# Perceiver layer kernel: attention energies and self scores in tensor tiles of 32 rows by 64 columns, self outputs made transposed, a new bank layout and new step orders

## The reference

```python
x = x + xattn(layernorm(x), ctx, ctx, mask, Wq, bq, Wk, bk, Wv, bv, Wo, bo)
#   energy = einsum('bhqd,bhkd->bhqk', Q, K) / sqrt(16); masked to -1e20
#   softmax(energy) @ V, heads side by side, @ Wo.T + bo
x = x + attn(layernorm(x), W_Q, W_K, W_V, W_O)
#   rope(q), rope(k); scores = einsum('bhqd,bhkd->bhqk', q, k) / sqrt(16), causal
#   softmax(scores) @ v, heads side by side, @ W_O.T
x = x + ffn(layernorm(x), router_w, w0_kernel, w1_kernel, wo_kernel)
#   top-2 gates, dispatch to 8 experts, gelu(x w0) * (x w1), @ wo, combine
```

## Time and profile before

| | |
|---|---|
| time, three runs | 659.47 us median (658.26 to 662.77) |
| span of the profiled execution | 666.9 us (its own device time is not listed apart) |
| mean granted TensorE clock | 0.928 of full speed |
| busy share of PE, DVE, ACT, POOL | 92%, 69%, 49%, 31% |
| one full step of four batches | 43.8 us |
| tail | 82 us |

### The profile page before, as it was taken

The page is one execution under the profiler, slowest core; times in us unless marked ns, Lnnn a source line. Parts: engine busy times, 40 slices in busy tenths (PEclk is TensorE's granted clock), DMA queues, the critical chain, the costliest instruction groups (busy, mean ns, idle before and its releaser), DMA issues.

```text
span 666.9 us, 14695 instructions
## 1 busy us (share of the span) xinstructions
PE 614.8 (92%) x4639; PEld 571.1 (86%) x4639; DVE 457.8 (69%) x1190; ACT 329.8 (49%) x836; POOL 208.0 (31%) x327
## 2 busy tenths in 40 slices
PE   2889999999999999999999889758999996999996
PEld 2868889899898898998988778748999996999995
DVE  3415667567776685677666755555999975999984
ACT  3336665545544545455444220335566655666662
POOL 0410221103113021021130210224666654666760
PEclk9989999989999999899998965656999998999998
DMA  8011111100001011010000070002555563645501
GB/s 266 24 47 34 32 33 33 32 18 30 21 17 31 16 31 31 16 31 0 0 1 1 8 247 0 0 1 95 161 189 159 161 212 106 191 158 191 160 1 63
DMA packets 38408, 47.51 MB, mean 71 GB/s; under 512 B 2414, under 2 KB 30036, under 8 KB 38356
## 3 DMA queue, kind: packets, MB, share of 16 engines
q1 hardware_dynamic: 38356, 46.82, 22.5%
HBM read 45.77 MB, written 1.05 MB: 70 GB/s over the span
## 4 chain that ended last, share of the span: by engine, by line
PE 82%; DVE 8%; ACT 4%; issue 4%; DMA 1%; SPq 0%; POOL 0%; DVEq 0%; ACTq 0%
PE bank L208 17%; PE bank L209 16%; PE bank L210 16%; PE bank L503 7%; PE bank L585 5%; PE bank L471 5%; PE bank L489 4%; PE bank L608 4%; PE bank L429 2%; PE bank L840 1%; ACT Pr L908 1%; PE bank L724 1%; PE bank L644 1%; DVE PT L1218 1%; DVE sc L1313 1%
## 5 line engine op out<-in xcount | busy, mean ns | idle before, releaser
L908 ACT ACTIVATE Pr<-Sc,nmax 128x257 f32<-128x257 f32 x128 | 64.2, 503 | 102.5 <-DVE nmax L1183 102.5
L208 PE MATMUL bank<-XT_lo,W_hi 128*128 (+1 forms) x352 | 101.5, 288 | 5.8 <-DVE W_lo L1523 4.4
L209 PE MATMUL bank<-XT_hi,W_lo 128*128 (+1 forms) x352 | 100.8, 286 | 0.0
L210 PE MATMUL bank<-XT_hi,W_hi 128*128 (+1 forms) x352 | 100.5, 286 | 0.0
L1697 POOL TENSOR_TENSOR W_lo<-raw,W_hi 128x256 fp32r<-128x256 f32 (+1 forms) x88 | 86.2, 979 | 7.0
L1523 DVE TENSOR_TENSOR W_lo<-raw,W_hi 128x512 fp32r<-128x512 f32 (+1 forms) x91 | 72.6, 802 | 5.0 <-ACT W_hi L1023 1.3
L1183 DVE CUSTOM_DVE_ANT_0 Sc<-bank,mask_add 128x257 f32<-128x257 f32 x128 | 49.2, 422 | 38.6 <-PE bank L471 37.4
L208 PEld LDWEIGHTS bank<-XT_lo,W_hi 128*128 128x128 f32 (+1 forms) x352 | 67.4, 191 | 6.4 <-issue 6.4
L1553 DVE TENSOR_TENSOR hid_lo<-hid,hid_hi 128x256 fp32r<-128x256 f32 (+1 forms) x88 | 69.3, 787 | 3.0 <-ACT hid_hi L1105 2.9
L209 PEld LDWEIGHTS bank<-XT_hi,W_lo 128*128 128x128 f32 (+1 forms) x352 | 67.3, 191 | 0.0
L210 PEld LDWEIGHTS bank<-XT_hi,W_hi 128*128 128x128 f32 (+1 forms) x352 | 67.1, 191 | 0.0
(11 more groups left out here) (210 smaller groups left out, 1572.1 us busy)
## 6 DMA issues: line engine op xcount, KB each, us to landing
raw<-in_L_ffn_w_kernel SPq DMA_DIRECT2D x32, 512.0 KB, 4.6
ctx_raw<-in_ctx SPq DMA_DIRECT2D x32, 256.0 KB, 2.7
raw<-in_L_ffn_wo_kernel SPq DMA_DIRECT2D x16, 512.0 KB, 5.7
raw<-in_L_ffn_w_kernel SPq DMA_DIRECT2D x16, 344.0 KB
raw<-in_L_ffn_wo_kernel SPq DMA_DIRECT2D x8, 256.0 KB
x_sb<-in_x SPq DMA_DIRECT2D x1, 1024.0 KB, 5.8
out<-fin SPq DMA_DIRECT2D x8, 128.0 KB, 1.8
raw<-in_L_ffn_wo_kernel SPq DMA_DIRECT2D x8, 88.0 KB
```

Source lines behind the costliest of these rows:

```text
L208: pe.matmul(dst, a_hi, b_lo, start=first, stop=False)
L209: pe.matmul(dst, a_lo, b_hi, start=False, stop=False)
L210: return pe.matmul(dst, a_hi, b_hi, start=False, stop=last)
L908: ac.activation(Pr[:, r % 2, g, 0:SC], Sc[:, r % 2, g, 0:SC], ACT.Exp, bias=nmax[:, r % 2, g:g + 1], scale=-1.0, accum_out=Pr[:, r % 2, g, ...
```

## The change

Five things change together.

1. **Energies.** HP = 2 heads per block of 32 rows. `energies(b, r)` issues all of a batch at once: 8 matmuls of 32 rows by 64 columns, into banks 0 to 3, two halves of the output partitions each. `Qb` is half as large.
2. **Scores.** The same tiles: 32 matmuls in one call, into columns 258 and up of banks 0 to 3 (`spare`). Half 0 of the probabilities and the turned self probabilities use the same columns, so PE waits before each of them until the last reader is done.
3. **Self outputs.** The values are padded with zeros to 32 columns (`Vm`) and used as weights, so the product comes out transposed; `turn_self` and `normalise` go. The probabilities are divided before they are turned: `add_probs` on VectorE (128x512 reduction and a reciprocal), `scale_probs` on GpSimd (128x512).
4. **Banks.** 0 to 3 energies and `spare`; 4 turned context and half 1; 5 keys and values both; 6 front; 7 back, and in its upper half the outputs.
5. **Orders.** Self probabilities are turned and spread at u = 3 instead of u = 2, self outputs are one call at u = 3; the tail has a new order. In the head, four weights are loaded in two transfers each.

```diff
         def values(b, r):
...
-            if beyond(b, 3):
-                pe.wait_ge(sm["o_read"], b - 2)
-            elif b > 0:
-                pe.wait_ge(sm["v_ready"], b)
+            pe.wait_ge(sm["k_ready"], b + 1)
...
-        def energies(b, r, pair):
+        def energies(b, r):
...
-            if beyond(b, 1) or pair:
-                pe.wait_ge(sm["s_read"], 4 * b + 2 * pair)
-            for g in range(2):
-                last = pe.matmul(bk[3 + g][:, 0:SC], Qb[64 * g:64 * g + 64, r % 2, pair, :, :],
-                                 KT[64 * g:64 * g + 64, r % 2, pair, 0:SC], start=True, stop=True)
...
+            if beyond(b, 1):
+                pe.wait_ge(sm["s_read"], 4 * b)
+            if beyond(b, 2):
+                pe.wait_ge(sm["pt0_ready"], b - 1)
+            for c in range(KH):
+                for g in range(G):
+                    rows = slice(S * g, S * g + S)
+                    last = pe.matmul(bk[g][64 * c:64 * c + 64, 0:SC], Qb[rows, r % 2, c, :, :], KT[rows, r % 2, c, 0:SC],
+                                     start=True, stop=True)
             last.then_inc(sm["s_made"], 1)
...
         def turn_probs(b, r, t):
...
                 pe.wait_ge(sm["p_ready"], 4 * b + 4)
+                pe.wait_ge(sm["s_read"], 4 * min(b + 2, B) if isinstance(b, int) else 4 * b + 8)
...
+        def outputs(b, r, t):
...
+            if exists(t, TT):
+                pe.wait_ge(sm[("b_x2", "c_yT", "c_lg", "b_x2")[(r + 2) % 4]], t + 1)
...
+            for b in range(BT):
+                for c in range(KH):
+                    for g in range(G):
+                        rows = slice(S * g, S * g + S)
+                        last = pe.matmul(spare(t)[64 * c:64 * c + 64, g, b * S:(b + 1) * S], qTb[rows, c, b, :, :],
+                                         kT[rows, c, b * S:(b + 1) * S], start=True, stop=True)
+            last.then_inc(sm["b_s_made"], 1)
...
+        def after_self(t, scored):
...
+            if scored:
+                pe.wait_ge(sm["b_scaled"], t + 1)
+            else:
                 pe.wait_ge(sm["b_pT_act"], t + 1)
                 pe.wait_ge(sm["b_pT_dve"], t + 1)
...
+            for k in range(KH):
+                for a in range(HP):
+                    for q in range(BT):
+                        h = NH // KH * k + HP * q + a
+                        last = pe.matmul(back(t)[S * q:S * q + S, k * P:(k + 1) * P],
+                                         values_of(t)[:, h // HP, 3 * DH * a:3 * DH * a + S], PTd[:, h // HG, h % HG, :, :],
+                                         start=a == 0, stop=a == HP - 1)
...
+                if u == 1:
+                    scores(j - 2)
...
+                if u == 3:
+                    self_outputs(j - 2)
                 values(b + 1, (u + 1) % 4)
...
-        def maxima(b, r, pair):
+        def maxima(b, r, pair, t):
...
+            if pair == 0 and r % 2 and exists(t, TT):
+                ve.wait_ge(sm["b_s_made" if r == 1 else "b_pT_made"], t + 1)
...
+        def add_probs(t):
...
+            ve.tensor_reduce(sum2[:, :], flat(pr2), X, ALU.add).then_inc(sm["b_sum"], 1)
+            ve.wait_ge(sm["b_sum"], t + 1)
+            ve.reciprocal(inv2[:, :], sum2[:, :]).then_inc(sm["b_inv"], 1)
...
+        def scale_probs(t):
...
+            po.tensor_tensor(probs, probs, inv2[:, :].unsqueeze(2).broadcast_to([P, NH, S]), ALU.mult).then_inc(sm["b_pn"], 1)
```

More of the change, by code:

```diff
@@ L51, in constants @@
     slot = np.broadcast_to(np.arange(E * CAP), (P, E * CAP))
-    parts = [ident, before, np.repeat(cos, 2, 1), sin, -sin, causal, block, expert, first_slot, slot]
+    parts = [ident, before, np.repeat(cos, 2, 1), sin, -sin, np.tile(causal, (1, BT)), block, expert, first_slot, slot]
     table = np.concatenate([np.asarray(t, np.float32) for t in parts], 1)
@@ L251, in halves, with weight_in, positions_at, spare @@
         return ap.rearrange("p (k n) -> p k n", k=KH)
+    def weight_in(i):
+        return 16 * KH if i in BY_HEAD else 16
     def front(t):
-        return bk[1] if isinstance(t, int) and t == TT - 1 else bk[2]
+        return bk[4] if isinstance(t, int) and t == TT - 1 else bk[6]
     def back(t):
-        return bk[5] if isinstance(t, int) and t == TT - 1 else bk[6]
+        return front(t) if isinstance(t, int) and t >= TT - 2 else bk[7]
+    def positions_at(k):
+        return bk[(7, 4)[k]]
+    def spare(t):
+        at_ = SC + 1 if not isinstance(t, int) or t < TT - 2 else 2 * P if t == TT - 2 else 3 * P
+        return bank[:, 0:G, at_:at_ + P]
     def values_of(t):
-        return Vs[:, int(isinstance(t, int) and t == TT - 1)]
+        return Vm[:, int(isinstance(t, int) and t == TT - 1)]
+    BY_HEAD = (0, 1, 4, 5)
     BATCHES = [(0, TT - 2), (TT - 2, TT)]
@@ L634, in turn_router @@
             pe.wait_ge(sm["c_y"], t + 1)
+            if back(t) is bk[7]:
+                pe.wait_ge(sm["o_read"], B if isinstance(t, int) and t == TT - 3 else BT * t + 3 * BT - 1)
             for k in range(KH):
@@ L711, in positions @@
             pe.wait_ge(sm["r_chosen"], k + 1)
-            pe.matmul(bk[0][:, 0:2 * n], before, chosen[:, :, t0:t1, :], start=True, stop=True)
-            pe.matmul(bk[0][:, 2 * n:3 * n], ones[:, :], chosen[:, 0, t0:t1, :], start=True, stop=True)\
+            if k == 0:
+                pe.wait_ge(sm["o_read"], B)
+            at_ = positions_at(k)
+            pe.matmul(at_[:, 0:2 * n], before, chosen[:, :, t0:t1, :], start=True, stop=True)
+            pe.matmul(at_[:, 2 * n:3 * n], ones[:, :], chosen[:, 0, t0:t1, :], start=True, stop=True)\
               .then_inc(sm["r_pos_made"], 1)
@@ L1655, in step @@
                 elif u == 2:
+                    scale_probs(j - 2)
                     power(j - 1, "b")
```

328 lines of the change are left out of this document (157 added, 171 removed).

## The result

| | before | changed |
|---|---|---|
| time, four runs each | 661.12 us (658.26 to 667.95) | 679.38 us (674.4 to 684.25) |
| the changed kernel again, second series | 662.44 us | 672.43 us |
| profiled span | 666.9 us | 672.6 us |
| mean granted clock in it | 0.928 | 0.933 |
| full step | 43.83 us | 44.48 us |

The change makes the kernel slower: the ratio is 1.025 (95% interval 1.0185 to 1.0308) in the first series and 1.016 (1.0106 to 1.0221) in the second. The forecast was 668 us with a range of 648 to 692. The eight runs of the changed kernel fall into two groups, five of 670.7 to 675.2 us at a granted clock of 0.933 to 0.946 and three of 683.1 to 684.3 us at 0.920 to 0.922, so that the median of 679.38 us is the middle between two and two; the profiled execution (674.4 us) is of the first group.

A forecast was written before the change was run, and what follows sets the result against it. PE was taken to bound the loop, as long as VectorE's and ScalarE's answers stay hidden. First batches +8, steps +3.6, tail -3 and head +0.5 gave +9 us, 668 us on the median; range 648 to 692.

The forecast's parts named there:

- The plain batch: Loop: stalls of 1.1 us before the transposes and 0.6 before the values make a batch 8.5 us, against 7.52.
- The full step: Four batches of the loop: 35.4 us of PE work plus 9.1 of stalls, 44.5 against 43.8; six steps +3.6.
- the 0.10 us that I charged for leaving the row tiles: Energies on PE: each pair of calls was taken to cost about 0.10 us extra for leaving the row tiles twice.
- Energies: PE, each batch: the new call takes 0.6 us, 0.75 with entering and leaving; 0.75 less per batch, 3.0 per step.
- Scores: PE, each step: 64 records in 1.6 us, bounds 0.9 and 6.8; 2.9 us less per step.
- self outputs: PE, each step: 32 records in 1.1 us with entering and leaving, instead of 3.5; 2.2 us less per step.
- Rival (b): PE tiles: column halves run one after the other, much slower, 690 to 704 us; chance 0.15.
- The first eight batches: Start of the loop: waits for maxima and key copy add 1.0 us to each batch, +8 us.
- The head: Before the loop: two more transfers ahead of biases and x delay the first matmul, +0.5 us, 0 to +1.5.
- The tail: After the loop: shorter scores and self outputs of z against new waits, about -3 us, from -8 to +1.
- Rival (a): Loop: VectorE's and ScalarE's answers stay hidden under PE work (covers hold), so faster, 645 us; chance 0.25.
- Rival (c): PE's clock: stalls drop it to 1.2 GHz in part of the loop, about 680 us; chance 0.10.

The follow-up runs named there:

- the context turned twice: Kernel before the change with each batch's four transposes of the context issued twice: 670.35 us, ratio 1.0097.
- the maxima together: Changed kernel with a batch's last two maxima on VectorE right behind its first two, ahead of split context and output copies: 630.29 us, ratio 0.9525.

## Why the prediction was right, point by point

**The direction and the mechanism were right.** The plain batch was forecast at 8.5 us with stalls of 1.1 and 0.6 us; it takes 8.70 with 1.14 and 0.4 (the transposes' own stretch is a little longer than I had it). The chain behind it is shown by four runs: cut it at the maxima and 42 us go, cut it at the key copy and 10 us go, lengthen PE's work off the chain and the step stays, lengthen it at the chain's head and the batch grows by as much.

**The full step** was forecast at 44.5 and is 44.48, which is luck in part, for two errors cancel: I had 35.4 us of work and 9.1 of stalls, and it is 36.76 and 7.7. The waits I listed are there but for the output projection's (0.3), most of them smaller: x of tile j-3 0.3 for 0.6, the transposes at u = 0 and u = 2 2.4 for 2.9, the cross projection's 0.5 for 0.7, the transposes at u = 1 1.1 for 1.4, keys' copies 0.6 for 1.0, the spread self probabilities 1.1 for 1.2; the q and k projection's is larger, 1.2 for 1.0. One I had not is the logits' (0.5 us for the output copies). Some of the surplus of work is a matter of counting: the last matmul ahead of a wait counts as 0.28 us of PE, one that is followed at once as 0.12. And the 0.10 us that I charged for leaving the row tiles isn't there: behind the transposes of the kernel before, which use the whole array, the first matmul of the values is as long (0.36 us, 89.34) as the first of the keys is behind the energies (0.38).

**Tiles.** Energies 0.62 us for a forecast of 0.6. Scores 0.84 for 1.6, a little under the lower bound of 0.9, and self outputs 1.08 for 1.1. Rival (b), column halves one after the other, did not happen. The rule in the Trainium skill ("TensorE: Matmul & The Clock Gate", Part 3, The mechanism) that a weight load overlaps matmuls only of another row group would have given 1.0 us or more for the energies and about 3.4 for the self outputs, whose four column tiles all use the same rows; the runs disagree with it as far as time goes: 0.62 us and 1.08. So they do with the estimate by the overhead per matmul that the Trainium skill gives ("TensorEngine Tiling (Array Packing)", Instruction Overhead; 1.6 us for 64 records): 64 records start within 0.84 us, so that overhead is not paid one after another across tiles.

**The first eight batches** were forecast at +8 and cost +10.6. Batch 0 alone costs 3.5 of it: it has no transposes ahead of its values, so its wait for the key copy is 2.7 us instead of 0.4, and behind that wait PE ran 3.6 us at the lower level of its clock (1.2 GHz; a granted clock of 0.53 in the second stretch).

```profile
56.63 0.39 PE L208 MATMUL bank<-WT_lo,ctxT_hi 128*128 128x256 f32 x1 [2.73 <-ACT KT L915]
```

```profile
56.63:57.40 0.77, 0.77 (x6) 0.77 (x7) 0.00 (x0) 0.00 (x0) 0.00 (x0) 1.00 0.00 0
57.40:61.00 3.60, 3.60 (x32) 3.17 (x31) 0.54 (x1) 1.51 (x3) 0.00 (x0) 0.53 0.02 5
61.00:69.42 8.42, 5.94 (x61) 5.07 (x45) 4.15 (x16) 4.92 (x15) 0.53 (x2) 1.00 0.10 32
```

The other seven cost 7.1, a microsecond each, as forecast. I had named the mechanism and not walked that batch.

**The head** is the term that was mis-sized: +0.5 with a bound of 1.5, measured +4.8 in this pair of executions (4.0 to 10.5 over all pairs of the two kernels' heads). I priced the two added transfers by their issues (0.46 us) and named the biases; the transfers themselves had changed shape, used a quarter of the engines and moved at a fifth of the rate. The bound was taken from the queue that issues, and not from the engines that carry.

**The tail** with the last step was forecast at -2.4 and gave -5.6. The term that was off most is z's scores, 3.3 us in the sum and 1.19 in the trace, to be held against the earlier trace rows; z's self outputs took 1.94 of the 2 forecast. The other 1.1 us I did not assign.

```profile
419.89 1.19 PE L621 MATMUL bank<-kT,qTb 32*64 32x32 f32 x64
```

**Rival (a)** (covers hold, 645) failed for the reason given against it: the split context and the output copies stand between the pairs. It became true when that order was changed, at 630. **Rival (c)** (clock) is partly there: the first two batches run at 0.90 where those of the kernel before have 1.00, and three of its eight runs are 10 us longer at a clock of 0.92. The steps at 0.96 (43.7 and 46.2 us) don't speak for it, since the kernel before has two of those as well, and with the context turned twice it has them with PE busy the whole time (46.60 us of 46.60).

The median of 679.38 us is 11 above the forecast, and 5 of that are the distance to the profiled execution (674.4). Up to the experts that one is 12.3 us longer than the kernel before, where the sum was +9: the head gives 4.3 more, the first batches 2.6, the steps 0.5 less and the tail 3.2 less. The longer runs go with a granted clock of 0.92; how much of the 11 us is the clock's no run here isolates. So the mechanism was right, and the total is near because the terms' errors partly cancel and the range was wide.

## What to carry to other kernels

When several tiles make all of a batch's results ready at once, the reader's order must change too: an order that was right for results in two portions turned 67 us of saved PE work into a loss of 10 to 18 us, and moving one line gave 42 back. To find such a place, walk one plain period with the other engines' times from the trace, and see whose last answer closes it. A move that cures one wait must be checked for who waits on everything it is put ahead of. A transfer that keeps its bytes but changes its shape is priced by its own rate, not by its issue.

## What the runs showed of the hardware

- fp32 matmuls of 32 rows by 64 columns in eight tiles ran side by side: 16 records of 257 columns in 0.62 us (four records in two tiles of 64 rows took 0.63), 64 records of 32 columns in 0.84 us; and 32 records of 128 columns in four column tiles on the same 128 rows took 1.01 us to the next instruction.
- Loading 256x256 fp32 in two transfers of 128 partitions by 1 KB whose source is four groups of 32 rows kept 2 tenths of the DMA engines busy, at 50 to 110 GB/s; with every weight in one transfer the same 4 us show 9 tenths at 320 to 410 GB/s (kernel before) and 6 to 9 tenths at 215 to 410 (changed kernel), until the weights are in. Changing the shape of four loads moved the first energies from between 49.5 and 53.1 us to 44.3.
- After 2.73 us in which PE stood still its clock stayed at the upper level for 0.8 us, was at the lower one (1.2 GHz) for 3.6 us and then back, with PE busy. With the maxima together, where the wait in that place is 1.5 us, the first two batches ran at 1.00. Full steps with 7.7 us of waits in pieces of at most 1.2 us kept 1.00 in three of the five.
